# A pre-norm decoder layer: both batches of x projected raw, mean and deviation applied behind the projection

## What is computed

```python
x = x + attn(layernorm(x), Wqkv, bqkv, Wo, bo)      # one head of width 256, softmax(q k' / 16) v Wo
x = x + xattn(layernorm(x), ctx, scales, zeros)     # fake-quantised x times fake-quantised ctx (2, 1024, 1024)
x = x + ffn(layernorm(x), c1, c2, w1, w2t)          # 56 blocks: argmax of a rank-16 score picks one row of each
layernorm(x) = (x - mean) / sqrt(var + 1e-5)
```

## Time and profile before

| what | us |
|---|---|
| median of 3 runs | 771.4 |
| lowest and highest run | 771.31 and 953.51 |
| the profiled execution | 771.97 |
| its span, first to last instruction | 770.0 |

### The profile page before, as it was taken

One profiled execution on the slowest core, in us unless ns is written; L12 is line 12 of the kernel. 1 busy time (PEld: TensorE's weight loads), 2 busy tenths in 40 slices (PEclk: granted clock), 3 DMA queues, 4 the chain that ended last, 5 costly groups with the idle time before them and its releaser, 6 DMA issues.

```text
span 770.0 us, 11457 instructions
## 1 busy us (share of the span) xinstructions
PE 761.8 (99%) x3586; PEld 624.2 (81%) x3586; DVE 610.9 (79%) x974; ACT 246.7 (32%) x378; POOL 468.2 (61%) x306
## 2 busy tenths in 40 slices
PE   8999999999999999999999999999999999999998
PEld 7888887468878888888888888888888888888887
DVE  5887769997887878888878788787888787778864
ACT  5348668794132030312122221203031212222120
POOL 4887798769997364645537363636464563736260
PEclk9999999999999999999999999999999999999999
DMA  8536406300222221222222222212122222222114
GB/s 313 214 113 215 168 6 157 59 14 1 69 68 69 66 60 32 68 75 68 75 68 68 73 70 68 68 45 61 51 68 75 68 75 68 68 68 68 61 38 195
DMA packets 59636, 64.19 MB, mean 83 GB/s; under 512 B 41312, under 2 KB 43616, under 8 KB 59360
## 3 DMA queue, kind: packets, MB, share of 16 engines
q1 hardware_dynamic: 59328, 62.75, 26.1%
q10 hardware_dynamic: 288, 1.18, 0.4%
HBM read 50.79 MB, written 4.19 MB: 71 GB/s over the span
## 4 chain that ended last, share of the span: by engine, by line
PE 92%; DVE 4%; ACT 2%; DMA 1%; issue 1%; SPq 0%; DVEq 0%; ACTq 0%
PE bank L1910 13%; PE bank L1911 13%; PE bank L1912 13%; PE bank L1810 12%; PE bank L1812 12%; PE bank L1811 12%; PE bank L1617 4%; PE bank L1619 4%; PE bank L1618 4%; PE bank L1801 2%; DMA x<-x_in 1%; DVE x L1301 1%; PE bank L1780 1%; DVE xn L1288 1%; ACT spread L774 1%
## 5 line engine op out<-in xcount | busy, mean ns | idle before, releaser
L1910 PE MATMUL bank<-w_hi,h_hi 128*128 128x512 f32 (+1 forms) x450 | 175.6, 390 | 0.0
L1911 PE MATMUL bank<-w_lo,h_hi 128*128 128x512 f32 (+1 forms) x450 | 175.3, 389 | 0.0
L1912 PE MATMUL bank<-w_hi,h_lo 128*128 128x512 f32 (+1 forms) x450 | 174.7, 388 | 0.0
L1414 DVE TENSOR_TENSOR x<-bank,x 128x512 f32<-128x512 f32 x207 | 132.8, 685 | 48.2 <-PE bank L1912 48.1
L636 POOL TENSOR_TENSOR lo_r<-r,slot 128x512 fp32r<-128x512 f32 x54 | 70.6, 1307 | 157.1 <-ACT slot L881 157.1
L1912 PEld LDWEIGHTS bank<-w_hi,h_lo 128*128 128x128 f32 x450 | 84.5, 188 | 18.0
L1910 PEld LDWEIGHTS bank<-w_hi,h_hi 128*128 128x128 f32 x450 | 84.5, 188 | 17.1
L1911 PEld LDWEIGHTS bank<-w_lo,h_hi 128*128 128x128 f32 x450 | 84.7, 188 | 15.1
L1810 PE MATMUL bank<-xT_hi,slot 128*128 128x512 f32 x232 | 90.5, 390 | 0.0
L1811 PE MATMUL bank<-xT_lo,slot 128*128 128x512 f32 x232 | 90.3, 389 | 0.0
L945 ACT ACTIVATE h_hi<-bank 128x512 fp32r<-128x512 f32 x56 | 33.3, 599 | 119.0 <-DVE bank L1355 81.4
(11 more groups left out here) (212 smaller groups left out, 1589.9 us busy)
## 6 DMA issues: line engine op xcount, KB each, us to landing
r<-w SPq DMA_DIRECT2D x56, 256.0 KB, 3.5
w_raw<-w SPq DMA_DIRECT2D x28, 512.0 KB, 4.0
x<-x_in SPq DMA_DIRECT2D x8, 512.0 KB, 10.9
ctx_raw<-ctx_in SPq DMA_DIRECT2D x8, 512.0 KB, 3.3
xn<-ctx_in SPq DMA_DIRECT2D x8, 512.0 KB, 4.4
out<-x SPq DMA_DIRECT2D x7, 512.0 KB, 2.6
W_raw<-wqkv SPq DMA_DIRECT2D x6, 512.0 KB, 11.0
xT_raw<-xT_in SPq DMA_DIRECT2D x1, 2048.0 KB, 20.0
```

The source lines that it names most:

```text
L1414: nc.vector.tensor_tensor(x[:, t, c], bank[unit_banks(g)[p]][:, :], x[:, t, c], ALU.add).then_inc(unit_added, 1)
L1910: nc.tensor.matmul(dst, h_hi[:, j, m], w2_hi[:, j, c], start=j == 0, stop=False)
L1911: nc.tensor.matmul(dst, h_hi[:, j, m], w2_lo[:, j, c], start=False, stop=False)
L1912: last = nc.tensor.matmul(dst, h_lo[:, j, m], w2_hi[:, j, c], start=False, stop=j == GJ - 1)
```

## The change

1. Both batches of x are loaded in transposed form and projected raw, without normalising: with W's columns w, deviation r and mean m, ((x - m) r) w = r (x w - m sum(w)). The T1 and R jobs, `first_values` and `norm_xT` go. `xT_raw` of batch 0 comes in five chunks of 1, 1, 2, 2, 2 parts of 128 (`K_CHUNKS`), the query and key weights in the same five, then the values' in two; TensorE does all four Q jobs of batch 0 chunk by chunk (`project_first_qk`).
2. The mean is taken off by a rank-one matmul with a contraction of 4 rows (`centre_qk`, `centre_v`): rows of means (`m_rows`) and negated column sums of the weights (`w_rows`, `wv_rows`), each split into high and low. The sums come from a transposed copy of the weights, a new input `wT_in` of 3 MB, summed by ScalarE (queries) and VectorE (keys, values); 8 transposes for each batch and 6 for the weight sums turn columns into rows (`spread_rows`, `spread_weight_sums`), and ScalarE copies them out.
3. The deviation is applied at the eviction: a multiplication of each Q bank by a row on VectorE (`scale_Q`), and a multiply-add for values.
4. `WARM` is 18 in place of 44. The scores of batch 0 come before V(1, 0). x tiles 4 to 7 are loaded last.
5. Orders on VectorE, ScalarE and GpSimd: statistics of tiles 4 to 7 and the first context tiles come behind the constants and both value evictions; `add_bo` is spread between the conversions; `cut_Wo` is moved ahead of tiles 12 to 15; those tiles are rounded behind the second set of probabilities. In the third sublayer a cut of c2 and of weights is made earlier.

```diff
-WARM = 44
+WARM = 18
...
-    jobs = both("T1", 0) + both("T1", 1) + both("T1", 2) + [("V", 0, 0)] + both("T1", 3)
-    jobs += [("V", 0, 1), ("Q", 0, 0), ("R", 0), ("Q", 0, 1), ("R", 1), ("Q", 0, 2), ("Q", 0, 3), ("V", 1, 0)]
+    jobs = [("Q", 0, c) for c in range(4)] + [("V", 0, 0), ("V", 0, 1)]
     jobs += [("S", 0, i) for i in range(4)]
-    jobs += [("Q", 1, c) for c in range(4)] + [("V", 1, 1)]
+    jobs += [("V", 1, 0)] + [("Q", 1, c) for c in range(4)] + [("V", 1, 1)]
...
+            load_xT0(0)
+            load_xT0(1)
+            load_W(1)
+            load_xT0(2)
+            load_W(2)
+            load_x(0)
+            load_xT0(3)
+            load_W(3)
+            load_x(1)
+            load_xT0(4)
+            load_W(4)
+            load_W(VALUE_CHUNK, VALUE_CHUNK + 1)
+            load_x(2, 3)
+            load_wT(0)
+            load_wT(1)
...
+            load_wT(2)
+            load_xT1(0, 1)
...
-            sp.wait_ge(mm_done, nth("Q", 0, 3) + 1)
+            sp.wait_ge(mm_done, nth("V", 0, 1) + 1)
```

GpSimd:

```diff
-            add_bo(0, 1, 2, 3)
-            lo_xT(0)
-            add_bo(4)
-            lo_xT(1)
-            add_bo(5)
+            lo_xT1(1)
+            add_bo(0)
+            lo_xT1(2, 3)
+            add_bo(1)
...
             convert_ctx(0, 1)
-            add_bo(6)
+            add_bo(2)
             convert_ctx(2, 3)
-            add_bo(7)
-            convert_ctx(4, 5, 6, 7)
+            add_bo(3)
+            convert_ctx(4)
+            add_bo(4)
+            convert_ctx(5)
+            add_bo(5)
+            convert_ctx(6, 7)
+            add_bo(6, 7)
             add_q2(0, 1)
             convert_ctx(8, 9, 10, 11)
             add_q2(0, 2)
             add_q2(0, 3)
-            convert_ctx(12, 13, 14)
+            cut_Wo()
             add_q2(0, 4)
-            convert_ctx(15)
-            cut_Wo()
+            convert_ctx(12, 13, 14, 15)
```

VectorE (the constants of the quantiser stand between the two parts), and the rank-one matmul:

```diff
+            scale_Q(0, 0)
+            scale_Q(0, 1)
             lo_Q(0, 0)
+            scale_Q(0, 2)
             lo_Q(0, 1)
+            scale_Q(0, 3)
             lo_Q(0, 2)
+            lo_Q(0, 3)
...
+            lo_V(0, 0)
+            lo_V(0, 1)
+            first_stats(4)
+            first_stats(5)
+            first_stats(6)
+            first_stats(7)
+            split_m_cols(1)
+            norm_scale(0, 4)
             round_ctx(0)
             round_ctx(1)
+            maxima(0)
+            inverse_sums(0)
...
+            def centre_qk(b, c):
+                pe.wait_ge(w_copied, 1)
+                pe.wait_ge(rows_copied, 2 * b + 2)
+                nc.tensor.matmul(job_bank("Q", b, c)[:, :], w_rows[0:4, c * P:(c + 1) * P], m_rows[0:4, :], start=False,
+                                 stop=True).then_inc(mm_done, 1)
```

More of the change, by code:

```diff
@@ L137, in decoder_layer @@
     xT_lo = [at(f"xT_lo{b}", 48 + 32 * b, [P, KD, SB], F32R) for b in range(NB)]
-    xT_raw = at("xT_raw", 80, [P, KD, SB], F32)
+    xT_raw = [at(f"xT_raw{b}", 48 + 32 * b, [P, KD, SB], F32) for b in range(NB)]
     W_hi = at("W_hi", 96, [P, 3, KD, HD], F32R)
@@ L693, in _ @@
                 norm3(t)
-            plain_lo(0, 1)
+            for i in range(1, 4):
+                plain_lo(0, i)
             lo_c2(0)
@@ new lines, in spread_weight_sums @@
+            def spread_weight_sums(i):
+                pe.wait_ge(w_cols_ready, i + 1)
+                if i == 1:
+                    pe.wait_ge(rows_copied, 1)
+                home = rows_bank[0] if i else job_bank("V", 0, 1)
+                for n in range(2 if i else 4):
+                    last = nc.tensor.transpose(home[0:4, n * P:(n + 1) * P], w_cols[:, 4 * i + n, :].bitcast(F32), id_f[:, :])
+                last.then_inc(w_spread, 1)
+            def centre_qk(b, c):
[3 more added lines that the diff above has]
+                                 stop=True).then_inc(mm_done, 1)
```

623 lines of the change are left out of this document (342 added, 281 removed).

## The result

The changed kernel takes 782.7 us (median of 4 runs), the kernel before in the same comparison 771.8 (median of 4). The ratio is 1.0139, with a 95% interval of 1.0127 to 1.0151: 10.9 us slower, where I had forecast 4.4 slower and a range up to 782.0. (One of the four runs of the kernel before took 953.51 us, and the profiled executions of e13_best and e14_act_cuts were some 5 us late at the head's end already, at 91.10 and 90.64: the ratio leaves out the first, and of the other two only distances within the execution are read.) The changed kernel's profiled execution spans 780.6 us against 770.0. So the sign was right, and the size was less than half of what came.

The account below looks back on a forecast made before the run. TensorE, busy 761.8 of 770.0 us, was taken as the bound, with GpSimd deciding the change. 4.2 + 0.7 - 0.5 = 4.4 us over 771.97 gave 776.4, less 0.6 for the median: 775.8 us, range 766.5 to 782.

Parts of the forecast that it names:

- Head: Stretch up to TensorE's first transpose of the probabilities: to end at 86.2 us instead of 88.7, 2.5 earlier.
- Input wait (1): TensorE's wait in the first projections for the third chunk of inputs: 0.4 + 0.7 = 1.1 us, bounds 0 and 3.
- VectorE's chain (3): VectorE from queries to first context tile: scalar steps 4 us, first reciprocal at 61.8, TensorE waiting 2.4, bounds 0 and 4.3.
- my count of its work: TensorE's work from first projection to last value projection: 77.3 us, so the head would end at 82.7 without waits.
- (2): Rows for batch 0 and weight sums in the head: ready before needed, sums near 35 to 36; hidden, bounds 0 and 2.
- Tile 11: Context tile where GpSimd waits for VectorE: converted 7.6 us behind the head's end, at 93.8.
- rival B: Slower still: all scalar steps held, roundings held by GpSimd, tile 11 at 98.2; 780.2 us, chance 0.23.
- The 43.9 us of queued work: GpSimd's queue from tile 11's conversion through the first correction add: ends at 137.7, first quantised-product add 6.0 us late.
- less 1.85 of slack, plus 0.7, less 0.5: After the late add: TensorE's slack 1.85 us, VectorE hands on 0.7 more, earlier weight cut and c2 save 0.5.
- A: Rival, faster: GpSimd not late, tile 11 converted by 87.8, TensorE keeps 4.9 us; 766.5 us, chance 0.22.
- C: Rival, hidden: the head's gain is just given back at Wo's low part or the add; 771.4 within 1, chance 0.17.
- D: Rival, clock: falls to 1.2 GHz after the shorter warm-up, forty wide matmuls at double step, 9 us; 785, chance 0.05.

Follow-up runs that it names:

- e13_best: e9_sums_split with e11_scale_first's edit, GpSimd's first low part of A before the eighth correction addition, and two ScalarE cuts behind its last q1 conversion: 773.84 us.
- e14_act_cuts: Changed kernel with only ScalarE's cuts for c2 and the fourth part of A put back behind the last q1 conversion: 782.66 to 787.66 us, ratio 1.0151.
- e1_bo_early: Changed kernel with GpSimd's additions of bo moved forward, those to tiles 2 and 3 into its idle stretch before the first conversion: 779.98 us.
- e4_bo_thin: Changed kernel with the additions of bo to tiles 2 to 7 covering 8 of 1024 columns: 778.64 us.
- e11_scale_first: Changed kernel with VectorE making the scale of rows 4 and 5 before the first add of the quantised product, not behind it: 779.79 us.
- e16_before_sum_twice: Kernel before the change, with GpSimd doing the first sum of the second batch's context twice: 772.06 us, ratio 1.0004.
- e5_sums_first: Changed kernel with GpSimd doing two accumulating sums before it waits for context 11: 779.33 us.
- e17_ctx_forward: e13_best with contexts 12 to 15 scaled and rounded one place earlier, first two Wo-product additions between and before the last roundings, ones_r behind them: 773.11 us.
- e10_cuts_late: e9_sums_split with GpSimd's low part of c1 moved behind the first correction addition and its first low part of A before the eighth: 773.74 us.
- e2_rounds_late: Changed kernel with VectorE rounding contexts 9 and 10 behind the low part of K of batch 1, not before it: 781.28 us.
- e6_both: e1_bo_early with three GpSimd sums also placed before the conversion of context 11: 776.79 us.
- e9_sums_split: e6_both with the last three sums of the first batch placed between GpSimd's conversions of contexts 11 to 14: 773.93 us.

## Why the prediction was wrong, by its own steps

**Head.** Forecast 86.2, measured 86.04, 2.5 earlier than before. The end was right by luck: three of its terms were not. Input wait (1): 1.1 forecast (whose 0.4 and 0.7 don't follow from the 10.9, 11.1 and 13.6 beside them), none came; the loads ran at 408 GB/s from 5.6 on. VectorE's chain (3): 4 us for the scalar steps and a wait of 2.4; they took 1.1 (41.60 to 42.73), with one of them held, for 0.41, until GpSimd's addition ended at 42.13, and GpSimd idle behind that; TensorE waited for nothing. In their place TensorE started at 5.6 and not 5.4, and my count of its work was 2 to 3 us short: 80.4 us from 5.60 to 86.04 without a wait, of which 0.9 are the four matmuls at the slow pace, against 77.3. The errors cancelled. (2) was right: the weight sums were ready at 31.3 and 34.2.

**Tile 11, the step that failed.** "That tile is converted 7.6 us behind the head's end": 93.8 forecast, 97.94 measured, 11.9 behind. The 7.6 had only one scaling of context, the low parts of the probabilities, a rounding of 0.7 and the conversion in it, and took VectorE to be through with everything else when the head ends. It wasn't: the held rounding of context 10 ran to 88.48, 2.4 us past the head's end, and the last cut of K and the values' eviction and cut stood behind it, so the low parts of the probabilities began at 93.66. Two roundings were held, for 2.69 and 2.62, beside a GpSimd without a pause. The run e1_bo_early, where they take 1.07 and 0.69, converts tile 11 at 95.2; e4_bo_thin at 93.9. The main sum had no holding at all, and rival B had the mechanism at 0.5 for each of five roundings, where these two lost 2.0 each; its 98.2 for tile 11 is near the 97.94, but by way of a head's end at 88.1 that didn't come. B went from the mean of the earlier trace rows, 1.34, against which 0.5 looks like much; that mean mixes roundings of 0.68 with held ones. What mattered was what GpSimd would be doing at that time, and I had moved three more additions of bo there myself.

**From tile 11 to the first add.** The 43.9 us of queued work were 45.2 (97.94 to 143.2), with 0.73 of idle time in them. With tile 11 that makes the add 11.6 late, not 6.0. The steps on the tail came out in sum: less 1.85 of slack, plus 0.7, less 0.5 would give 10.0, and the spans differ by 10.6. That is luck in part. The sum has no term for the waits for q1T, which are worth 2.3 to 2.6 (the rest of e11_scale_first is 634.7, not 637.3); without them the rest would be 3.6 shorter than before the change, not 1.65, so the lateness was absorbed by more than I gave it. That the kernel before had slack on GpSimd, e16_before_sum_twice shows; the 1.85 on TensorE no run tested by itself.

**Rivals.** A falls, since tile 11 was not converted by 87.8, and C, since the loss is 10.9. B was nearest, with 780.2 and most of its mechanism. D falls as it was put: of its forty wide matmuls at double the step four came, worth 0.9. The granted clock did fall, to a mean of 0.80 between 136.3 and 144.8, but behind TensorE's own wait there, where it next waited for the add in any case (in e1_bo_early the clock is 1.00 there, and TensorE waits 1.7 for the add in place of 0.2). Of my signs of right and wrong, the projection stream's end near 28 (28.3), GpSimd's idle time near 50 to 57 (49.9 to 55.4) and the two waits on GpSimd were there; the wait on VectorE at 48 to 62 was not, nor did the one-element steps end with a low part of GpSimd's.

**Not foreseen.** The waits of 2.3 for q1T, a consequence of the late add (e11_scale_first). The scale stood behind the same add in the kernel before too, but there the add was on time. And I took GpSimd's order as given: its queue held 5.5 us of idle time that no sum was allowed to fill, and e5_sums_first got 3.4 of them back by moving one line.

**Left open.** e17_ctx_forward is 1.3 us slower than the kernel before (1.0015), with the head's end 2.4 us earlier (86.10). Its profile shows TensorE's waits of 0.4 (for the low part of the values), 1.1 and 1.2 in the stretch in which this lead is lost; that without them it would beat the kernel before was not tried, and the two edits made to find it (e10_cuts_late, e13_best) brought nothing. No version faster than the kernel before was found.

## What to carry to other kernels

When a change makes one engine earlier, the engine that was just behind it decides, and its queue has to be written anew: put in front of each wait for a late tile the work that doesn't need it. An estimate of when a tile comes needs what the neighbouring engine does at that very time, not the mean of a group over the whole stretch. And find the one instruction that all later work follows (here VectorE's first add of the quantised product): its start, counted from a point that the edit can't touch, tells what an edit did to the time with a precision that no sum of waits has, since TensorE's waits are moved along as often as they are removed.

## What was not expected of the hardware

A rounding of 128x1024 (one SBUF input) took 0.68 us alone and up to 4.99 beside GpSimd (102.35 to 107.34, while GpSimd's low part of Wo ran from 102.25 to 106.80). It did not run at half the pace, it waited for the end of GpSimd's instruction: the three held ones of the changed kernel end at 85.93, 88.48 and 107.34, and GpSimd's instructions beside them at 85.38, 87.92 and 106.80, 0.54 to 0.56 earlier each time. The adds with one input in PSUM took 1.27 us (125.75) beside GpSimd's 14.24 us of sums, and 1.28 again in the middle of them (130.27): they were not held. The Trainium skill ("SBUF — State Buffer", section "SBUF: two separate sides") has it as an exclusive lock, taken for a whole instruction by GpSimd or by a VectorE instruction in a two-port mode or with two SBUF inputs, the latter only against a GpSimd instruction that reads SBUF. These rows agree that the wait is for the whole instruction, and that adds with one SBUF input pass. That a rounding, with one SBUF input too, runs in a two-port mode no row says; that it is held, these do. I had used the rule only for the one-element steps, of which this time one was held, for 0.41 us.

The pace of TensorE's first matmuls differs between executions of the same instructions. In the profiles of the changed kernel, e1_bo_early, e4_bo_thin and e5_sums_first the first four wide ones take 0.44 to 0.46 us each, in those of e2_rounds_late, e6_both and e9_sums_split 0.25, with the same 18 transposes ahead. It is worth 0.8 us, and these can stay until the head's end: the projections of queries and keys end at 28.30 in the changed kernel and at 27.48 in e2_rounds_late, and the heads at 86.04 and 85.22. In e6_both, where the first matmuls are fast, a wait of 0.3 for a low part of the weights came near 13 us, and the head ended at 86.11. So a gain of under 1 us in one profile can be the head's, and the 3.89 us of slow transposes in the earlier trace rows are no constant to plan a start by.
